# Ternary expert weights stored as bfloat16 rows and transposed by DMA, in place of TensorE transposes and fp8 storage

## What is computed

```python
x = x + tanh(g_xattn[0]) * readout(layernorm(x), ctx, mask)
x = x + tanh(g_ffn[0])   * L0_ffn(layernorm(x), router_w, wg, wu, wd)
x = x + tanh(g_xattn[1]) * L1_xattn(layernorm(x), ctx, Wq, Wk, Wv, Wo, ...)
x = x + tanh(g_ffn[1])   * L1_ffn(layernorm(x), w1, b1, w2, b2)

# L0_ffn: one of 8 experts per token, picked by argmax of x @ router_w.T
def _weight_quant(w):
    s = 1.0 / clip(mean(abs(w)), EPS, None)
    return clip(round(w * s), -1.0, 1.0) / s
g = bitlinear(xf, wg[e]);  u = bitlinear(xf, wu[e])      # xq @ wq.T
y = bitlinear(square(relu(g)) * u, wd[e])
```

## Time and profile before

| what | us |
|---|---|
| median of 3 runs | 1642.63 |
| lowest, highest | 1638.80, 1645.27 |
| the profiled execution | 1641.37 |
| its span | 1639.6 |
| TensorE busy in the span | 1409.4 |
| VectorE busy | 1132.4 |
| ScalarE busy | 950.4 |
| GpSimd busy | 524.4 |

### The profile page before, as it was taken

How to read it: one execution, slowest core, us unless ns; L and a number is a source line. 1 busy time by engine, 2 the same in 40 slices (tenths; PEclk the granted TensorE clock), 3 DMA queues, 4 the chain that set the end, 5 groups by cost and what they waited for, 6 DMA issues and landing times. The chain is left out here.

```text
span 1639.6 us, 26673 instructions
## 1 busy us (share of the span) xinstructions
PE 1409.4 (86%) x9883; PEld 851.5 (52%) x9959; DVE 1132.4 (69%) x1444; ACT 950.4 (58%) x1440; POOL 524.4 (32%) x401
## 2 busy tenths in 40 slices
PE   4999996999942794779999999999795899999996
PEld 3555453555422352323776776775233666666663
DVE  4788856578873596838778788786576676565561
ACT  5788843445433595423777777777623866665651
POOL 0122210000053005314999999997520000000000
PEclk8999998999965896876999999999897899999998
DMA  6688761000028438430353443542481876656640
GB/s 232 222 288 305 249 218 40 1 1 1 1 81 342 136 125 204 107 90 4 67 105 85 86 98 71 104 113 81 99 287 52 295 255 231 207 204 211 220 145 27
DMA packets 162674, 233.22 MB, mean 142 GB/s; under 512 B 46396, under 2 KB 80191, under 8 KB 161416
## 3 DMA queue, kind: packets, MB, share of 16 engines
q1 hardware_dynamic: 157064, 206.60, 41.8%
q0 software_dynamic: 5504, 25.20, 4.2%
HBM read 169.62 MB, written 55.65 MB: 137 GB/s over the span
## 5 line engine op out<-in xcount | busy, mean ns | idle before, releaser
L1726 POOL TENSOR_TENSOR t_low<-t_e 128x1024 bf16<-128x1024 f32 x185 | 365.0, 2001 | 48.1 <-ACT t_e L1773 48.1
L1811 DVE TENSOR_REDUCE t_nmax<-t_psM 128x1 f32<-128x1024 f32 x256 | 309.5, 1221 | 75.0 <-PE t_psM L1894 73.6
L1773 ACT ACTIVATE t_e<-t_psE 128x512 f32<-128x512 f32 x512 | 277.9, 595 | 105.0 <-PE t_psE L1916 97.5
L1894 PE MATMUL t_psM<-kst,qst 96*64 96x512 bf16 x1024 | 189.0, 406 | 14.0 <-DVE t_nmax L1811 7.0
L2411 PE MATMUL e_psG<-late_flat,e_w1p 128*128 (+1 forms) x1536 | 172.3, 275 | 13.7 <-DVE e_hT L2355 9.1
L1916 PE MATMUL t_psE<-qst,kst 99*64 99x512 bf16 x1024 | 181.9, 386 | 1.3
L2411 PEld LDWEIGHTS e_psG<-late_flat,e_w1p 128*128 128x128 bf16 x1536 | 151.3, 99 | 35.2 <-issue 8.3
L1930 PE MATMUL t_psO<-t_e,vst 128*33 128x512 bf16 x768 | 163.9, 392 | 3.7 <-POOL t_low L1726 3.7
L2426 PE MATMUL e_psO<-e_w2p,e_hT 128*128 128x512 bf16 x752 | 164.9, 379 | 0.8
L1894 PEld LDWEIGHTS t_psM<-kst,qst 96*64 96x64 bf16 x1024 | 89.0, 113 | 77.8 <-DVE t_nmax L1811 35.0
L2426 PEld LDWEIGHTS e_psO<-e_w2p,e_hT 128*128 128x128 bf16 x768 | 75.0, 98 | 89.0
(11 more groups left out here) (268 smaller groups left out, 2376.4 us busy)
## 6 DMA issues: line engine op xcount, KB each, us to landing
piece<-in_L_ffn_w SPq DMA_DIRECT2D x32, 1024.0 KB, 13.8
xres<-in_L_ffn_w SPq DMA_DIRECT2D x32, 1024.0 KB, 14.8
wT<-ternary POOLq DMA_DIRECT2D x8, 1536.0 KB
kst<-keys SPq DMA_DIRECT2D x96, 128.0 KB, 3.5
c_rows<-in_ctx SPq DMA_DIRECT2D x8, 1024.0 KB, 9.4
xres<-in_L_ffn_wg SPq DMA_DIRECT2D x8, 1024.0 KB, 6.1
xres<-in_L_ffn_wu SPq DMA_DIRECT2D x8, 1024.0 KB, 6.8
xres<-in_L_ffn_wd SPq DMA_DIRECT2D x8, 1024.0 KB, 6.2
```

Of the source, the lines that this page charges most:

```text
L1726: nc.gpsimd.tensor_tensor(low[:, low_slot(h, u), :, :], e32[:, slot(h, u), :, :], upper(h, u), ALU.subtract).then_inc(lo_pool, 1)
L1773: nc.scalar.activation(e32[:, slot(h, u), i, :], psE[:, i, :], ACT.Exp, scale=SC).then_inc(expd, 1)
L1811: nc.vector.tensor_reduce(nmax[:, h // G % 2, h % G, u:u + 1], banks_of(place_of_max(b, m)).rearrange("p a t -> p (a t)"), AX_X, ALU.max, ...
L1894: last = nc.tensor.matmul(banks_of(place_of_max(b, m))[side * SIDE:(side + 1) * SIDE, i, :], qst[0:KR, g, h % G, s0:s0 + SIDE], kst[0:KR, ...
```

## The change

VectorE's third pass still writes bfloat16 rows into tern. TensorE's transposes of them, ScalarE's copies, the PSUM tile psW and the fp8 tile wout go. POOL stores each matrix as it is, 512 rows of 512 bfloat16, 512 KB in one DMA, as soon as it is cast; the cast of matrix i waits for the store of matrix i-2. The DRAM tensor is bfloat16. In the router stage SyncE in place of POOL loads the weights, with 32 transposing DMAs: for each expert four, each with all 1536 rows (gate, up, down) and 128 of the columns, which land as 128 partitions x 1536. Those of the first two experts are issued ahead of the zero store, the last two experts' after it has landed. SyncE waits for all of them at the end of the stage. In wT an expert is now laid out by column block and then row, and weights_of reads 512 elements in a row.

```diff
-    AFTER_SUM, AFTER_TERN = 2, 5
+    AFTER_SUM, AFTER_STORE = 2, 4
     w32 = xres[:, 0:3 * QD, :].rearrange("p (s k) d -> p s k d", k=KC)
-    tern = xres[:, 3 * QD:, :].rearrange("p k d -> p (k d)").bitcast(BF16).rearrange("p (s k d) -> p s k d", s=2, k=KC)
+    tern = xres[:, 3 * QD:, :].rearrange("p k d -> p (k d)").bitcast(BF16).rearrange("p (s k d) -> p s k d", s=WR, k=KC)
...
-        wout = sb("c_wout", [P, WR, KC, 2 * P], mybir.dt.float8e4)
...
-        psW = c.enter_context(nc.psum_tensor("c_psW", [P, 2, KC, P], BF16))
...
-        w_xposed, w_copied = sem("c_w_xposed"), sem("c_w_copied")
...
-        def half_at(s):
-
-            return s - AFTER_TERN if 0 <= s - AFTER_TERN < 2 * NW else None
...
-                for h in range(2 * NW):
-                    i, r = divmod(h, 2)
-                    pool.wait_ge(w_copied, h + 1)
-                    nc.gpsimd.dma_start(wt_dram[i // 3, :, i % 3, r, :, :],
-                                        wout[:, h % WR, :, :]).then_inc(w_stored[h % WR], 16)
+                for i in range(NW):
+                    pool.wait_ge(cast, i + 1)
+                    nc.gpsimd.dma_start(wt_dram[i // 3, i % 3].rearrange("(u p) d -> p u d", p=P),
+                                        tern[:, i % WR, :, :]).then_inc(w_stored[i % WR], 16)
                 for r in range(WR):
-                    pool.wait_ge(w_stored[r], 16 * (2 * NW // WR))
+                    pool.wait_ge(w_stored[r], 16 * (NW // WR))
...
                     if b < 3:
                         sp.wait_ge(cast, NW - 2 + b)
                     else:
-                        sp.wait_ge(w_xposed, 2 * NW)
+                        for r in range(WR):
+                            sp.wait_ge(w_stored[r], 16 * (NW // WR))
...
-                        if s == 2 * NW + (1, 1, 1, AFTER_TERN)[b]:
+                        if s == 2 * NW + (1, 1, 1, AFTER_STORE)[b]:
...
-                def w_copy(h):
-                    act.wait_ge(w_xposed, h + 1)
-                    if h >= WR:
-                        act.wait_ge(w_stored[h % WR], h // WR * 16)
-                    nc.scalar.copy(wout[:, h % WR, :, :].rearrange("p k (u s) -> p u k s", s=P), psW[:, :, :, :],
-                                   saturate=True).then_inc(w_copied, 1)
...
-                        if (h := half_at(s)) is not None:
-                            w_copy(h)
                         if s % 2 == 0 and s // 2 < NW:
                             total(s // 2)
...
-                    if i >= 2:
-                        dve.wait_ge(w_xposed, 2 * i - 2)
-                    v.tensor_scalar(tern[:, i % 2, :, :], w32[:, m, :, :], -MAGIC, None, ALU.add).then_inc(cast, 1)
+                    if i >= WR:
+                        dve.wait_ge(w_stored[i % WR], i // WR * 16)
+                    v.tensor_scalar(tern[:, i % WR, :, :], w32[:, m, :, :], -MAGIC, None, ALU.add).then_inc(cast, 1)
...
-                def w_transposes(h):
-                    i, r = divmod(h, 2)
-                    pe.wait_ge(cast, i + 1)
-                    if h >= 1:
-                        pe.wait_ge(w_copied, h)
-                    for u in range(2):
-                        for k in range(KC):
-                            last = nc.tensor.transpose(psW[:, u, k, :], tern[:, i % 2, 2 * r + u, k * P:(k + 1) * P], ident[:, :])
-                    last.then_inc(w_xposed, 1)
...
-                        if (h := half_at(s)) is not None:
-                            w_transposes(h)
                         gemm(q, n)
...
-                for e in range(E):
-                    if e == E - 2:
-                        pool.wait_ge(zero_stored, 16)
-                    nc.gpsimd.dma_start(wT[:, e, :, :, :, :].rearrange("p m r k d -> p (m r k d)"),
-                                        wt_dram[e].rearrange("p m r k d -> p (m r k d)")).then_inc(w_fetched, 16)
                 pool.wait_ge(placed, 3)
...
                 pool.wait_ge(scattered, 16 * NT)
-                pool.wait_ge(w_fetched, 16 * E)
...
             @block.sync
             def _(sp):
+                def load_turned(e):
+                    for k in range(KC):
+                        sp.dma_start_transpose(wT[:, e, k, :],
+                                               wt_dram[e].rearrange("m o d -> (m o) d")[:, k * P:(k + 1) * P]
+                                               ).then_inc(w_fetched, 16)
+
                 sp.wait_ge(consts, ROWS_ZERO)
                 sp.dma_start(rows[0:E, :], router_w).then_inc(router_loaded, 16)
+                for e in range(2):
+                    load_turned(e)
                 sp.wait_ge(zero_set, 1)
                 sp.dma_start(dispatch_dram.rearrange("(p n) d -> p (n d)", p=P),
-                             wT[:, E - 2:E, :, :, :, :].rearrange("p e m r k d -> p (e m r k d)")[:, 0:NS * DW].bitcast(F32)).then_inc(zero_stored, 16)
+                             wT[:, E - 2:E, :, :].rearrange("p e k o -> p (e k o)")[:, 0:NS * DW].bitcast(F32)).then_inc(zero_stored, 16)
+                for e in range(2, E - 2):
+                    load_turned(e)
+                sp.wait_ge(zero_stored, 16)
+                for e in range(E - 2, E):
+                    load_turned(e)
+                sp.wait_ge(w_fetched, 16 * KC * E)
...
-                    return lambda m, k: wT[:, bass.ds(e, 1), m, :, k, :].rearrange("p o r d -> p (o r) d")
+                    return lambda m, k: wT[:, bass.ds(e, 1), k, m * D:(m + 1) * D].rearrange("p o d -> p (o d)")
...
-    wt_dram = dram("ternary", (E, P, 3, 2, KC, D // 2), mybir.dt.float8e4)
+    wt_dram = dram("ternary", (E, 3, D, D), BF16)
...
-                wT = moe.enter_context(nc.sbuf_tensor("wT", [P, E, 3, 2, KC, D // 2], BF16))
+                wT = moe.enter_context(nc.sbuf_tensor("wT", [P, E, KC, 3 * D], BF16))
```

More of the change, by code:

```diff
@@ L806, in _ @@
                 done(nc.gpsimd.tensor_tensor(rstd[:, :], veps[:, :], half[:, :], ALU.pow))
-                nc.gpsimd.memset(wT[:, E - 2:E, :, :, :, :], 0.0).then_inc(zero_set, 1)
+                nc.gpsimd.memset(wT[:, E - 2:E, :, :], 0.0).then_inc(zero_set, 1)
                 pool.wait_ge(zero_set, 1)
```

## The result

The kernel after takes 1653.53 us in the median of 4 runs (1649.1 to 1654.83), the kernel before 1643.91 beside it (4 runs): ratio 1.0063, 95% interval 1.0038 to 1.0089, so about 10 us slower. The profiled execution took 1649.1 us (span 1647.4).

A forecast was written before the change was run, and what follows sets the result against it. The prediction took weight loads to pace the context stage and the scatters to set the router stage's end. Context +2.0 and router +1.6 gave +3.6 us on 1642.63, so 1646 us, range 1630 to 1690.

The forecast's parts named there:

- B: Router stage: transposed loads outlast the scatters, each over 1.94 us; 1667 us at 150 GB/s, 1709 at 100; chance 0.33.
- A: Likeliest case: weight loads keep the context stage's pace, transposed loads hidden or nearly; 1646 us, range 1635 to 1651; chance 0.42.
- What sets the pace: Context stage: weight loads, not busy TensorE, set the lap from one cast to that two tensors on, averaging 14.43 us.
- The context stage: Weight-making stage: laps +4.2 us from larger stores, -2.2 us from transposes gone after the last load-bound cast; together +2.0 us.
- 0.40: Context stage: average growth per load, 13 loads at +0.79 us and 8 at -0.24; +4.2 us over 10.5 laps.
- the other 8: Context stage: of 21 slot reloads, those where ScalarE did not wait; removing its copy saves up to 1.03 us each.
- towards 30: Context stage: ScalarE's total wait for weight loads was to grow from 9.8 us towards 30.
- The tail: Context stage after the last load-bound cast: five transpose groups of 0.44 us leave TensorE's path, -2.2 us.
- The router stage: 32 transposed loads at 198 GB/s take 63.5 us, plus a 9.3 us zero store, ending at 542.0: +1.6 us.
- The two signs given for B: Router stage: DMA activity beyond 545 with POOL and PE idle; zero store issued much later than 482.7, holding the scatters.
- C: Context stage gets TensorE's relief: laps fall to 13.3 us, 14 us saved with the tail, 1629 us; chance 0.12.
- D: Context stage slower by itself: store ahead of load, +14 us, or TensorE loses its clock; 1657 us; chance 0.07.

The follow-up runs named there:

- half_after: Kernel after with each weight load from the fourth matrix on bringing 512 KB in place of 1024 KB, passes kept full size: 1629.86 us, ratio 0.9903.
- half_before: Kernel before with each weight load from the fourth matrix on bringing 512 KB in place of 1024 KB: 1635.6 us, ratio 0.9946.
- back: Kernel after with TensorE's transposes and ScalarE's copies put back beside the new store, their result not stored or used: 1651.88 us, ratio 1.0069.
- swap_before: Kernel before with ScalarE evacuating its bank before it sums the next matrix: 1647.59 us, ratio 1.0031.
- zero_before: Kernel before with the router stage's zero store reading a small zero tile of 520 bytes per partition 46 times: 1652.35 us, ratio 1.0069.
- zten_before: Kernel before with only 2392 bytes per partition zeroed and the zero store reading that piece ten times: 1633.92 us, ratio 0.9934.
- plain: Kernel after with the 32 transposing loads replaced by ordinary ones of the same bytes in 3072-byte runs, nothing transposed: 1644.56 us, ratio 1.0004.
- short: Kernel after with the 32 transposing loads replaced by ordinary ones in 256-byte runs, nothing transposed: 1647.53 us, ratio 1.0028.
- zten_after: Kernel after with only 2392 bytes per partition zeroed and the zero store reading that piece ten times: 1650.3 us, ratio 1.0035.
- double: Kernel after with each ternary matrix stored twice, the second time into a spare DRAM tensor: 1670.84 us, ratio 1.0152.
- late: Kernel after with each ternary store held back until the load taking the matrix's old slot has landed: 1665.09 us, ratio 1.0127.
- swap_after: Kernel after with ScalarE evacuating its bank before it sums the next matrix: 1650.57 us, ratio 1.0055.

## Why the prediction was right, and where it was not

The time, 1653.5, lies in the range (1630 to 1690), and both terms of the sum have the right sign. But the likeliest case said 1646 and a difference within 0.5%, with a range of its own up to 1651; the runs say +0.63%. So two terms were too small, together by some 5 us, most of it in the router stage. The wide range holds the time because it was drawn around B as well; A's own range does not hold it.

**What sets the pace: right.** That the weight loads and not the busy TensorE set it was read from the timeline, and half_after, half_before and back bear it out. In the kernel before it held by less than I thought: TensorE's own work was 13.47 us a lap (158.72 of 170 us, times 14.43), and shorter loads gain only 0.5 us. swap_before, where no wait for a load is left and no lap is shorter, says that the loads' hold on that kernel was not ScalarE's wait alone.

**The context stage: +2.0 forecast, +3.6 measured** (a_xn at 261.04 in the mean of before, zero_before and zten_before, at 264.68 in that of after, plain, short and zten_after, whose context stages are the same). Single profiles of these kernels lie at 259.54 to 262.52 and at 262.55 to 265.84, so 3.6 is good to about 2 us and the miss of 1.6 isn't clear of that. The laps grew by 0.53 us (14.38 to 14.91 in the same means), not 0.40, again no more than the scatter of single profiles (14.22 to 14.50, and 14.74 to 14.98).

That 0.40 was near is in part luck: it was 0.79 for the bytes less 0.39 for the relief (8 x 1.03 / 21). In back, which has the bytes and not the relief, a lap is 14.83, so by that one profile the bytes cost 0.45 and the relief gave nothing. The step that failed is "in the other 8 the copy stood just ahead of the sum, so up to 1.03 us each": where ScalarE copies no more it waits for the load instead, 20 or 21 times in all four kernels with the context stage of after and 16 times in back, against 13, 16 and 12 in before, zero_before and zten_before. For that reason the wait, forecast "towards 30", came out at 59.5. The price of the bytes itself, 0.79, is near the 0.87 of double, but that holds where every lap waits for its load; the laps of before seem to have had some room.

The tail was smaller than forecast. From the last cast to a_xn it is 45.5 us in every kernel with the context stage of before and 43.8 in every one with that of after:

```profile
261.06 0.55 DVE L552 TENSOR_SCALAR a_xn<-xres,moments,a_rstd 128x512 f32<-128x512 f32 x1 [4.27 <-POOL a_rstd L478]
```

```profile
264.93 0.55 DVE L524 TENSOR_SCALAR a_xn<-xres,moments,a_rstd 128x512 f32<-128x512 f32 x1 [3.95 <-POOL a_rstd L450]
```

261.06 - 215.60 is 45.46, 264.93 - 221.13 is 43.80: -1.7 us, not -2.2. In back it is 45.1, so this is the one place where the relief shows. The rest of the difference between eleven laps of 0.53 and 3.6 us lies ahead of the second cast and is scatter.

The stores landed in 7.8 us in the median, not near the 4.4 of the earlier trace rows: those were 128 KB each, and the new ones are four times that, not twice. No cast waited for one, as forecast.

**The router stage: +1.6 forecast, +5.2 measured** (71.45 in the mean of before, swap_before and half_before, 76.70 in that of after, back, double, late, swap_after and half_after). The price per load was right: 1.96 us at 201 GB/s, where I had 1.99 from 198 GB/s. That a rate taken from other transfers, in another stage and not transposed, came so near is partly luck; short shows the run length to be most of it. The sum for the queue was right up to the last issue: 63.5 + 9.3 = 72.8 us forecast, and from 474.67 to the end of the last issue, 548.00, it is 73.3. What failed is the comparison: I set this end against the first row load of the mixture, 540.43, and had no term for what follows the last issue. In the profile after, 3.25 us lie between the last issue's end and that row load (548.00 to 551.25): 2.6 until the last load has landed and 0.6 after. Rival B's mechanism was thus the true one in this stage, with A's price. Its condition, "each must take over 1.94 us", should have been lowered by those 3 us: (62 - 3.25) / 32 = 1.84, below my own estimate of 1.99; 32 times the difference is 4.8 us. The two signs given for B both came: DMA activity beyond 545 with POOL and PE idle, and a zero store issued later than before, though at 489.99 it held nothing.

The Trainium skill (Advanced Engine Details and Errata, X-Bar Transpose) says 350 to 400 GB/s for transposed DMAs; the trace shows 201. Its page VectorE: DVE Perf Modes (The three transpose paths) speaks of 1309 ns for a tile by DMA; here a load of 12 tiles took 1.96 us, so they are not done one after another at that price.

**C, faster, fell** because the waits for the loads took up the relief. half_after reached 13.26 us, the 13.3 that C named, but with half of the bytes; that the two figures agree is chance, as C's was the shortest lap of a loop with whole loads.

**D was half there.** The granted clock did fall in the context stage, to 0.79 from 170 to 180 us, after a load of 9.7 us and, behind it, a wait of TensorE of 4.53 us:

```profile
177.06 0.56 PE L353 MATMUL c_psA<-c_absum,c_onesf 128*128 128x1 f32 x2 [4.53 <-DVE means L276]
177.48 7.87 PE L345 MATMUL c_psG<-c_wT,ctxT 128*128 128x512 bf16 x24
```

24 matmuls took 7.87 us, 0.33 each, where the earlier trace rows have 47 in 10.52, 0.22 each: 2.5 us of matmul more in this place. (0.79 is a mean over the stretch of the two levels, 2.4 and 1.2 GHz.) It fell once more, to 0.83 from 200 to 210 us. The kernels with the same context stage differ in this, as zten_after and then plain show:

```profile
50.00:220.00 170.00, 138.03 (x781) 67.86 (x779) 142.75 (x197) 90.56 (x125) 17.57 (x23) 1.00 0.87 297
```

```profile
50.00:220.00 170.00, 142.90 (x757) 69.60 (x770) 140.74 (x194) 90.53 (x123) 17.59 (x23) 0.93 0.86 293
```

At 1.00 the lap is 14.74 us, at the 0.97 of after 14.94, at the 0.93 of plain and of short 14.96 and 14.98. So the laps grow without any loss of clock, from 14.38 to 14.74. Up to 0.2 of the 0.53 us may be the clock's; single profiles scatter by more than that at a clock of 1.00 (14.22 to 14.50), so whether it is stays open.

## What to carry to other kernels

Before work is taken off an engine, find out whether anything waits for it, and let half of the suspected transfer's bytes tell: if the loop shortens, as here by 1.68 us a lap, relief for the engines is worth little, and bytes added to the loop cost time. When one chain is compared with the end of a stage, count on both sides what comes after the last transfer. Price a transfer by the length of its runs and not by its bytes alone: here the same bytes moved at 400 GB/s in runs of 3072 bytes and at 213 in runs of 256. Such a transfer is hidden only as long as the work beside it is slow.

## What was not expected of the hardware

A VectorE pass was held for as long as a memset of POOL's ran beside it: in the router stage of the kernel before, a pass over 128 x 512 float32 takes 10.64 us beside the 10.34 us memset of 128 x 12288 bfloat16, and 0.53 without it. Whether the memset was slowed too, no run shows. It is the dearest line of that stage, and a memset of 0.60 us in its place gave 10 us back.

```profile
472.38 10.34 POOL L807 MEMSET wT<- 128x12288 bf16 x1
...
472.35 10.64 DVE L881 TENSOR_SCALAR r_xn<-xres,moments,r_rstd 128x512 f32<-128x512 f32 x1 [0.52 <-POOL r_rstd L806]
```

Runs of 256 bytes about halve what the full DMA engines move: 213 GB/s in short against 400 in plain, where the runs are 3072 bytes, and with the transposition 201. The same 3 MB of zeros landed in 9.3 us as one run of 23920 bytes per partition, in 12.5 us in runs of 2392, and in 52.4 us in runs of 520. Each landed beside weight loads in part, and the last beside all eight of them, so that figure is no price of the runs alone.
